# W2's row sums built in PSUM, the sums and bias steps of batches 2 and 3 moved in VectorE's and TensorE's order, TensorE's loop written out

## The reference

```python
hidden = concatenate([cond, cond], axis=-1)
x_mean = mean(x, axis=1, keepdims=True)
fused  = concatenate([x, x_mean * ones_L, hidden[:, None, :] * ones_L], axis=-1)
out    = x + relu(einsum('bld,do->blo', fused, W) + b)
```

## Time and profile before

| | |
|---|---|
| median of 3 runs | 103.64 us (103.46 to 104.13) |
| profiled execution | 103.63 us |
| its span | 101.7 us |
| TensorE busy | 97.2 us, 96% |
| TensorE weight loads | 78.5 us, 77% |
| VectorE busy | 83.0 us, 82% |
| ScalarE busy | 47.1 us, 46% |
| GpSimd busy | 38.9 us, 38% |

### The profile page before, as it was taken

One profiled execution on the slowest core, in us unless ns is written; L12 is line 12 of the kernel. 1 busy time (PEld: TensorE's weight loads), 2 busy tenths in 40 slices (PEclk: granted clock), 3 DMA queues, 4 the chain that ended last, 5 costly groups with the idle time before them and its releaser, 6 DMA issues.

```text
span 101.7 us, 1713 instructions
## 1 busy us (share of the span) xinstructions
PE 97.2 (96%) x523; PEld 78.5 (77%) x523; DVE 83.0 (82%) x148; ACT 47.1 (46%) x116; POOL 38.9 (38%) x35
## 2 busy tenths in 40 slices
PE   5989999999999999999999999999999999999980
PEld 2348999988888786888888886888888886888870
DVE  3172789899899899999999984999999993996670
ACT  3285435895418279496397001874744003710000
POOL 1029800000000002999848500568578059950000
PEclk9999999999999999999999999999999999999999
DMA  1999999999999998999999388000591690299994
GB/s 38 269 303 290 273 268 282 273 251 266 318 256 231 269 251 221 246 234 226 345 331 286 106 195 219 0 0 0 113 267 32 134 259 20 67 283 273 248 325 144
DMA packets 35438, 21.39 MB, mean 210 GB/s; under 512 B 2020, under 2 KB 33128, under 8 KB 35432
## 3 DMA queue, kind: packets, MB, share of 16 engines
q1 hardware_dynamic: 33848, 20.13, 77.4%
q10 hardware_dynamic: 1584, 1.18, 3.9%
HBM read 12.91 MB, written 8.39 MB: 209 GB/s over the span
## 4 chain that ended last, share of the span: by engine, by line
PE 90%; DMA 4%; ACT 1%; DVE 1%; ACTq 0%; issue 0%
PE ps_y L472 77%; PE ps_y L573 4%; PE ps_y L575 4%; PE ps_y L574 4%; DMA xa<-in_x_dram 4%; PE ps_mean L491 1%; PE ps_const L540 1%; ACT xh L267 1%; DVE ps_xt L341 1%; ACT w1h L260 1%; DVE w L462 0%; ACTq L160 0%; PE ps_y L596 0%
## 5 line engine op out<-in xcount | busy, mean ns | idle before, releaser
L240 POOL TENSOR_TENSOR xa<-xa,back 128x512 f32 (+1 forms) x26 | 33.5, 1318 | 44.7 <-DVE back L354 44.7
L472 PE MATMUL ps_y<-xh,w1h 128*128 (+2 forms) x128 | 43.6, 368 | 0.4 <-ACT w1h L260 0.3
L472 PE MATMUL ps_y<-xl,w1h 128*128 (+2 forms) x128 | 43.0, 363 | 0.0
L472 PE MATMUL ps_y<-xh,w1l 128*128 (+2 forms) x128 | 42.8, 363 | 0.0
L267 ACT ACTIVATE xh<-ps_xt 128x512 fp32r<-128x512 f32 (+1 forms) x36 | 19.7, 549 | 17.4 <-DVE ps_xt L341 17.4
L472 PEld LDWEIGHTS ps_y<-xh,w1h 128*128 128x128 f32 x128 | 22.6, 189 | 5.4 <-issue 1.1
L347 DVE TENSOR_TENSOR xl<-ps_xt,xh 128x512 fp32r<-128x512 f32 (+1 forms) x36 | 22.1, 617 | 4.9 <-ACT xh L267 4.9
L472 PEld LDWEIGHTS ps_y<-xh,w1l 128*128 128x128 f32 x128 | 22.6, 189 | 3.8
L472 PEld LDWEIGHTS ps_y<-xl,w1h 128*128 128x128 f32 x128 | 22.7, 189 | 3.6
L341 DVE STREAM_TRANSPOSE ps_xt<-xa 128x512 f32<-128x512 f32 (+1 forms) x36 | 22.3, 642 | 3.6 <-DMA xa<-in_x_dram 3.3
L285 ACT ACTIVATE relu_t<-ps_y,bias 128x512 f32<-128x512 f32 x20 | 13.5, 686 | 16.8 <-DVE bias L388 15.3
(11 more groups left out here) (35 smaller groups left out, 37.1 us busy)
## 6 DMA issues: line engine op xcount, KB each, us to landing
xa<-in_x_dram SPq DMA_DIRECT2D x60, 128.0 KB, 3.8
out_dram<-xa SPq DMA_DIRECT2D x28, 256.0 KB, 4.1
w<-in_L_cond_W_dram SPq DMA_DIRECT2D x4, 256.0 KB, 5.5
w<-in_L_cond_W_dram SPq DMA_DIRECT2D x2, 512.0 KB, 6.7
w<-in_x_dram SPq DMA_DIRECT2D x4, 256.0 KB, 4.6
out_dram<-w SPq DMA_DIRECT2D x3, 256.0 KB, 3.4
xa<-in_x_dram ACTq DMA_DIRECT2D x4, 128.0 KB, 4.4
w<-in_L_cond_W_dram SPq DMA_DIRECT2D x4, 64.0 KB, 3.4
```

Source lines behind the costliest of these rows:

```text
L240: nc.gpsimd.tensor_tensor(rows, rows, back[:, t], ALU.add).then_inc(added, 1)
L472: return nc.tensor.matmul(ps_y[:, t, ls], lhs, rhs, start=start, stop=stop, skip_group_check=True)
```

## The change

Four edits:

- The four column sums are added one by one (four 128x1 adds with one tensor and one pointer operand each) and the row sums of W2 are built in PSUM's `ps_const`; only the last step writes `w2x` in SBUF. `const_product`, which writes the same bank, waits for batch 0's sums.
- On VectorE, batch 2's sums come before the turn-back of tile 11 (with the split of n = 11 ahead of them), and its bias step behind the turn-back of tile 12; batch 3's sums come behind the turn-back of tile 20, and its bias step before that of tile 22.
- On TensorE, batch 3's mean product comes inside tile (6, 2), behind its first 3 of 12 matmuls, instead of behind the tile.
- TensorE's hardware loop over halves 3 to 6 is written out.

```diff
--- before.py
+++ after.py
@@ -130,7 +130,8 @@
 
         ps_xt = psum("ps_xt", [P, XT_BANKS, NL])
         ps_y = psum("ps_y", [P, Y_BANKS, NL])
-        ps_const = psum("ps_const", [P, NL])
+
+        ps_const = psum("ps_const", [P, D])
         ps_mean = psum("ps_mean", [P, NL])
 
         x0_landed = [sem(f"x0_landed{h}") for h in range(2)]
@@ -363,12 +364,16 @@
                 else:
                     dve.wait_ge(mean_done, b)
                     dve.wait_ge(w2x_step, NK * b)
-                nc.vector.tensor_tensor(bsum[:], xsum[:, H * b + 1], xsum[:, H * b + 2], ALU.add).then_inc(bsum_ready, 1)
-                dve.wait_ge(bsum_ready, b + 1)
-                nc.vector.tensor_scalar(w2x[:], w2[:, 0], bsum[:, 0:1], None, ALU.mult).then_inc(w2x_step, 1)
+                for k in range(NK):
+                    nc.vector.tensor_scalar(bsum[:, k:k + 1], xsum[:, H * b + 1, k:k + 1], xsum[:, H * b + 2, k:k + 1], None,
+                                            ALU.add).then_inc(bsum_ready, 1)
+                dve.wait_ge(bsum_ready, NK * b + 1)
+                nc.vector.tensor_scalar(ps_const[:], w2[:, 0], bsum[:, 0:1], None, ALU.mult).then_inc(w2x_step, 1)
                 for k in range(1, NK):
+                    dve.wait_ge(bsum_ready, NK * b + k + 1)
                     dve.wait_ge(w2x_step, NK * b + k)
-                    nc.vector.scalar_tensor_tensor(out=w2x[:], in0=w2[:, k], scalar=bsum[:, k:k + 1], in1=w2x[:],
+                    sums = w2x if k == NK - 1 else ps_const
+                    nc.vector.scalar_tensor_tensor(out=sums[:], in0=w2[:, k], scalar=bsum[:, k:k + 1], in1=ps_const[:],
                                                    op0=ALU.mult, op1=ALU.add).then_inc(w2x_step, 1)
 
             def last_rows(step, r, y, cols):
@@ -426,16 +431,25 @@
             for n in range(len(tiles)):
                 if n == 2:
                     sum_bias(1)
-                elif n == NK * (H + 1):
+                elif n == NK * H * (B - 1) - 2:
+                    sum_bias(B - 1)
+                if n == NK * (H + 1) - 1:
+
+                    x_low(n_x)
+                    n_x += 1
+                    mean_terms(2)
+                turn_back(n)
+                if n == NK * (H + 1):
                     sum_bias(2)
-                elif n == NK * H * (B - 1):
-                    sum_bias(B - 1)
-                turn_back(n)
                 if n >= len(tiles) - DVE_ADDS:
                     g, t = tiles[n]
                     rows = xa[:, g, :, Q * t:Q * t + Q]
                     dve.wait_ge(turned_back, n + 1)
                     nc.vector.tensor_tensor(rows, rows, back[:, t], ALU.add).then_inc(late_added, 1)
+                if n == NK * (H + 1) - 1:
+                    continue
+                if n == NK * (2 * H + 1):
+                    mean_terms(B - 1)
                 for _n in range(steps_of_x(n, 3)):
                     if n % NK == 0:
                         turn_x(n_x)
@@ -443,8 +457,6 @@
                         turn_x(n_x + 1)
                     x_low(n_x)
                     n_x += 1
-                if n // NK + SLOTS - 1 < G and n // NK > 0 and n // NK % H == 0 and n % NK == NK - 1:
-                    mean_terms(n // NK // H + 1)
 
             dve.wait_ge(last_bias_landed, 16)
             dve.wait_ge(last_x_landed, 16 * NR)
@@ -479,6 +491,10 @@
 
             def tile(g, slot, t):
                 for k in range(NK):
+                    if g == LAST - 1 and t == 2 and k == 1:
+
+                        pe.wait_ge(bias_ready, B - 1)
+                        mean_bias(B - 1)
                     if t == 0:
                         pe.wait_ge(xl_ready, pieces_to(g) + k + 1)
                     last = product(slot, k, t)
@@ -533,6 +549,8 @@
             def const_product():
 
                 pe.wait_ge(cond_spread, 1)
+
+                pe.wait_ge(w2x_step, NK)
                 pe.wait_ge(w3_landed, 16 * 2)
                 for r in range(2):
                     for k in range(CK):
@@ -556,16 +574,13 @@
                     pe.wait_ge(bias_ready, 1)
                     mean_bias(1)
 
-            with pe.Fori(1, B - 1) as b:
+            for g in range(H + 1, LAST):
                 for t in range(NK):
-                    pe.wait_ge(relu_done, NK * H * b + t + 1)
-                    tile(H * b + 1, (H * b + 1) % SLOTS, t)
-                for t in range(NK):
-                    pe.wait_ge(relu_done, NK * (H * b + 1) + t + 1)
-                    tile(H * b + H, (H * b + H) % SLOTS, t)
-                    if t == 2:
-                        pe.wait_ge(bias_ready, b + 1)
-                        mean_bias(b + 1)
+                    pe.wait_ge(relu_done, NK * (g - 1) + t + 1)
+                    tile(g, g % SLOTS, t)
+                    if g % H == 0 and g < LAST - 1 and t == 2:
+                        pe.wait_ge(bias_ready, g // H)
+                        mean_bias(g // H)
 
             def last_product(y, k, r, cols_h, cols_l, start, stop):
                 rows = slice(P * r, P * r + P)
```

## The result

| | before | after |
|---|---|---|
| median of 16 runs each | 103.42 us (103.11 to 104.13) | 104.65 us (104.23 to 105.5) |
| span of the profiled execution | 101.7 us | 102.9 us |

The account below looks back on a forecast made before the run. TensorE, 96% busy, was taken as the bound; 103.63 us for the profiled execution plus 0.1 for batch 1's product and 0.1 for batch 3's gave 103.8 us, range 103.2 to 104.4.

Parts of the forecast that it names:

- m: Length that the new form adds to each set of sums on VectorE: 0.3 us, between 0 and 0.7.
- The adds: Four small VectorE adds instead of one of 0.16 us: 0.1 to 0.5 us more, taken as 0.25.
- The first step: First row-sum step of each set, now written to PSUM: 0 to 0.2 us more, taken as 0.15.
- The other three: Later three row-sum steps of each set: 2.33 us kept or down to 2.15, taken as 0.1 less.
- Batch 1's product: TensorE's wait for batch 1's sums: m + (m - 0.2) - 0.31, taken as 0.1 us; 0.9 for m = 0.7.
- Batch 3's product: TensorE's wait at the mean product moved into tile (6, 2): 0 to 0.3 us, taken as 0.1.
- Rival 1: GpSimd's add holds the first step of batch 3's sums; TensorE waits 1.1 us there, 104.8 us in all; chance 0.10.
- Rival 2: TensorE's hardware loop did cost; writing it out returns 0.45 us of disturbance, 103.2 us; chance 0.04.
- Rival 3: Earlier stores clear the queues ahead of the last store, 0.1 to 0.3 us: 103.4 us; chance 0.06.
- Forecast case: The main prediction: small waits at batch 1's and batch 3's products, 103.8 us; chance 0.80.
- The const product's wait: TensorE's new wait for batch 0's sums in PSUM: 4 us of cover remain, so 0.
- the bias step of batch 3: VectorE's step moves from 84.78 to about 82.9, about 2 us earlier; priced at 0.

Follow-up runs that it names:

- mixed_behind: The changed kernel with the old form of sums for batches 0 and 1 and batch 3's mean product behind all of tile (6, 2): 104.33 us, 1.0065 of before.

## Why the prediction was wrong

**The step that failed is the size of m.** The prediction had "So m is 0.3 us, between 0 and 0.7"; it is 0.77, outside even its own bounds.
- The adds were taken at 0.25 more, and cost 0.29: right. The lower end of 0.06 apart stood on no row.
- The first step was taken at 0.15 more with 0.2 as the upper end, from the 0.69 us of a split; it costs 0.25 to 0.27, since this form takes 0.74 to 0.75.
- The other three were taken at 0.1 less. They are no shorter, and 0.21 longer by the wait for a second semaphore, which was in the diff and in the order, and which the prediction didn't price at all. It took the hand-over at 0.04 as on every row where one semaphore is waited for.

**Batch 1's product.** The formula m + (m - 0.2) - 0.31 was the right mechanism: with 0.77 it gives 1.03, and 1.24 was measured. Of the other 0.2, 0.13 are TensorE's arriving at 39.15 instead of 39.28. The prediction put 0.1.

**Batch 3's product.** "TensorE waits between 0 and 0.3 us; I take 0.1": it waited 0.43. VectorE takes 4.40 us from the turn-back at 79.27 to the end of the sums at 83.67, where the working had 82.23 - 78.14 = 4.09; the 0.3 more is the same error in m, and made up 0.3 of the wait's 0.35 too much. The rest held: TensorE's matmul ahead of the product starts 3.79 us behind the time at which VectorE can begin that turn-back, forecast and measured (81.93 - 78.14, 83.06 - 79.27).

**The range.** 0.9 + 0.3 waited gave 104.8 in the working, above the median that came; the range was then cut to 104.4 and the largest m left out, on belief and no row. With both ends of m in it, the range would have held the result, but by luck: m lay beyond its end, the waits were 1.67 us and not 1.2, and 0.35 of them cost nothing. The chance of slower could not have been 0.09.

**Rival 1, held by GpSimd: refuted.** The first step beside GpSimd takes 0.74 us as alone. Slower came, but by batch 1's sums, as the prediction's last part allowed ("m is near its upper end").

**Rival 2, the loop: wrong in sign.** Neither TensorE's pitch nor a gap changed; alone, the written-out loop costs 0.8% by one more code transfer that meets the stores. "Its removal gives 0" fits after, where by the trace the transfer is over (86.7 + 1.05) before the stores begin at 88.29; that is luck, since the prediction had no code transfer in it, and after with the loop kept wasn't run. The Trainium skill, Runtime: NRT & Kernel Launch, section Instruction fetch mechanics, says that code is refilled in 16 KiB blocks of 256 instructions and that this is mostly hidden; the size agrees with the packet here, and hidden it was wherever it didn't last into the first of the last stores.

**Rival 3, the tail: the number came, the mechanism only in part.** The tail is 0.35 us shorter, against 0.1 to 0.3 given. But the stores didn't go out earlier: the first is at 88.29, before's at 87.58. The last step was later still, so that the stores no longer decided. The working also put an earlier bias of batch 3 at 0 because "nothing in the tail waited for these except through TensorE"; with two turn-backs of half 5 moved behind the bias step, the stores do wait for it, and it decides by over a microsecond in `mixed_behind`. Forecast case and rival 3 weren't exclusive.

**What was right.** The const product's wait is free; batch 2's product doesn't wait; the bias step of batch 3 at 84.29 is the forecast 82.9 plus the 1.13 us by which VectorE there is late (79.27 for 78.14) and the 0.3 of the longer sums; the small adds take 0.54 us for four both beside GpSimd and alone, some 0.11 apart, as the "about 0.1 us each" said, and are not held.

## What to carry to other kernels

Price an edit's waits as well as its instructions: here a second semaphore on each of three dependent steps cost nearly as much as moving the sums to PSUM (0.21 and 0.27 us). Where work on a busy engine has a lead of a few tenths over the engine that sets the end, count each edit as often as it stands ahead of the meeting point, and doubt the lead itself. When all engines are done and the DMA engines still run, look at when the first of the last stores went out and at what else used the queues ahead of it, code transfers included.

## What the hardware showed that I had not expected

- A VectorE step that waits for two semaphores starts 0.11 us behind the one ahead instead of 0.04; the second wait is an instruction of its own (1737 against 1725 on the page).
- A step with a pointer scalar takes 0.75 us for 128x512 float32 with its running sum in SBUF or in PSUM alike; without the running sum it is 0.49 from SBUF to SBUF and 0.74 to PSUM.
- Three old steps beside GpSimd's add take 3.24 instead of 2.33 us; with the sums in PSUM the step beside it takes 0.74, as alone.
- A 16 KB code packet took 1.29 us of one DMA engine, which right ahead of the last stores made the kernel 0.8% longer; some 4 us earlier it cost nothing that could be measured.
